# A fused state-space layer: gate by tile over 512 tokens, C scaled by decay before the state's product, the squares' product a step later, the normed sequence kept in DRAM

## What is computed

```python
xn   = layernorm(x)                                   # x: [2, 1024, 512]
proj = xn @ in_proj_w.T                               # gate 4096, x 4096, B 8*128, C 8*128, dt 64
xBC  = silu(causal_conv(proj[x, B, C], 4 taps) + conv_bias)
dt_p = softplus(dt + dt_bias);  dA = exp(-dt_p * exp(A_log))
for t in range(1024):                                 # 64 heads of 64, state 64 x 128 each
    state = state * dA[t] + (dt_p[t] * x[t]) * B[t]
    y[t]  = state @ C[t] + D * x[t]                   # 8 heads share one B and one C
yn   = y * rsqrt(mean(y**2 over 512) + eps) * norm_weight * silu(gate)
s    = yn @ out_proj_w.T
g    = silu(xn @ (W + lora).T + bias)
out  = x + s * g
```

## Time and profile before

| | before |
|---|---|
| median of 3 executions | 1965.25 us (1963.15 to 1968.01) |
| the profiled execution, its own time | 1964.76 us |
| its span, first to last instruction | 1963.0 us |
| granted TensorE clock, mean | 0.983 |
| TensorE (PE) busy | 1849.3 us, 94% |
| VectorE (DVE) busy | 1628.2 us, 83% |
| GpSimd (POOL) busy | 1119.6 us, 57% |
| ScalarE (ACT) busy | 825.4 us, 42% |
| DMA | 185.16 MB, mean 94 GB/s |

### The profile page before, as it was taken

The page is one execution under the profiler, slowest core; times in us unless marked ns, Lnnn a source line. Parts: engine busy times, 40 slices in busy tenths (PEclk is TensorE's granted clock), DMA queues, the critical chain, the costliest instruction groups (busy, mean ns, idle before and its releaser), DMA issues.

```text
span 1963.0 us, 31108 instructions
## 1 busy us (share of the span) xinstructions
PE 1849.3 (94%) x11576; PEld 1527.0 (78%) x11576; DVE 1628.2 (83%) x2000; ACT 825.4 (42%) x1814; POOL 1119.6 (57%) x1145
## 2 busy tenths in 40 slices
PE   7968999999999999999897999999999999999997
PEld 5756888888888887878775888888888888788885
DVE  6758888888888888888875988888888888888896
ACT  4854343444435343434423434443443535344431
POOL 4125555664756555665665756565565555566467
PEclk9988999999999999999998999999999999999998
DMA  6232214242232224232244331314223221423233
GB/s 212 86 100 72 88 50 134 65 118 72 74 103 81 86 65 121 79 113 77 77 154 130 102 103 53 115 65 119 81 79 105 81 83 53 135 65 97 66 91 123
DMA packets 142566, 185.16 MB, mean 94 GB/s; under 512 B 11856, under 2 KB 89040, under 8 KB 142416
## 3 DMA queue, kind: packets, MB, share of 16 engines
q1 hardware_dynamic: 141376, 183.02, 30.9%
q10 hardware_dynamic: 1040, 0.16, 0.0%
HBM read 173.17 MB, written 9.97 MB: 93 GB/s over the span
## 4 chain that ended last, share of the span: by engine, by line
PE 53%; DVE 19%; issue 12%; POOL 9%; ACT 4%; DMA 2%; SPq 0%; POOLq 0%; DVEq 0%; ACTq 0%
PE ps_conv L1086 8%; PE ps_conv L1089 7%; DVE xc L746 5%; PE ps_conv L1092 5%; PE ps_gate L1089 3%; PE ps_gate L1086 3%; PE ps_y L1243 3%; PE ps_out L1086 3%; PE ps_out L1089 3%; DVE decay L854 3%; PE ps_s L1236 3%; PE ps_gate L1092 2%; PE ps_cs L1215 2%; PE ps_out L1092 2%; DVE ycs L834 2%
## 5 line engine op out<-in xcount | busy, mean ns | idle before, releaser
L746 DVE SCALAR_TENSOR_TENSOR xc<-ps_conv,convw_sb,xc 128x511 f32<-128x511 f32 (+2 forms) x576 | 429.7, 746 | 22.6 <-ACT xc L542 9.0
L914 DVE TENSOR_TENSOR decay<-decay,ps_s 128x1024 f32<-128x1024 f32 x128 | 156.0, 1219 | 210.5 <-PE ps_s L1272 210.4
L854 DVE TENSOR_TENSOR_SCAN decay<-decay,eye 128x1024 f32<-128x1024 f32 x128 | 327.8, 2561 | 1.0 <-DMA decay<-decays_d 1.0
L654 ACT ACTIVATE square<-ps_y 128x512 f32<-128x512 f32 x128 | 76.7, 599 | 511.8 <-DVE ps_y L872 511.8
L548 ACT ACTIVATE xc<-xc 128x512 f32<-128x512 f32 x192 | 121.3, 632 | 400.6 <-DVE xc L746 400.3
L1047 POOL TENSOR_TENSOR state<-state,total_bc 128x512 f32<-128x512 f32 x96 | 101.6, 1059 | 316.9 <-DVE state L861 176.5
L1026 POOL TENSOR_TENSOR skip<-skip,ycs 128x512 f32<-128x512 f32 x112 | 150.1, 1340 | 231.6 <-DVE ycs L834 228.8
L1086 PE MATMUL ps_conv<-xn_hi,wconv_hi 128*128 128x512 f32 x768 | 229.3, 420 | 12.4 <-ACT xn_hi L596 10.3
L1089 PE MATMUL ps_conv<-xn_hi,wconv_lo 128*128 128x512 f32 x768 | 209.7, 395 | 0.0
L1031 POOL TENSOR_TENSOR rstd_col<-mean_square,half 128x1 f32<-128x1 f32 x128 | 183.4, 1433 | 0.0
L1243 PEld LDWEIGHTS ps_y<-decay,dtx 128*64 128x64 f32 x2048 | 109.2, 136 | 90.8 <-issue 90.8
(11 more groups left out here) (199 smaller groups left out, 4064.2 us busy)
## 6 DMA issues: line engine op xcount, KB each, us to landing
decay<-decays_d SPq DMA_DIRECT2D x128, 512.0 KB, 5.1
stage<-w_in_t SPq DMA_DIRECT2D x32, 1024.0 KB, 6.4
prefix_bc<-rows_d SPq DMA_DIRECT2D x224, 128.0 KB, 4.8
stage<-w_out_t SPq DMA_DIRECT2D x16, 1024.0 KB, 6.9
stage<-w_in_t SPq DMA_DIRECT2D x32, 256.0 KB, 3.3
out_sum<-hidden SPq DMA_DIRECT2D x16, 256.0 KB, 4.8
ffn_d<-sgate SPq DMA_DIRECT2D x16, 256.0 KB, 2.0
next_x<-hidden SPq DMA_DIRECT2D x16, 256.0 KB, 4.1
```

The source lines that it names most:

```text
L746: e.scalar_tensor_tensor(acc[:, d:], ps[:, 0:BLK - d], convw_sb[:, tile, TAPS - 1 - d:TAPS - d], acc[:, d:], ALU.mult, ALU.add).then_inc(S ...
L854: e.tensor_tensor_scan(d[:, :], d[:, :], eye8[:, :, :].rearrange("p h i -> p (h i)"), 0.0, ALU.mult, ALU.add).then_inc(S["scan"], 1)
L914: e.tensor_tensor(by_head(d[:, :]), by_head(d[:, :]), ps_s[:, 0:P].unsqueeze(1).to_broadcast([P, GH, P]), ALU.mult).then_inc(S["M"], 1)
```

## The change

- **Gate**: one call is one channel tile over 512 tokens, 12 matmuls of 512 columns, with the weights split by channel tile. Step 0 makes four calls, then each step one, until the last at step 124. `sgate` is one buffer of 4 x 4 tiles, written by channel tile and read by chunk; the two roles of its axes alternate.
- **State's product**: GpSimd multiplies the fetched prefix rows (broadcast to all 128 partitions for 8 heads) by C, 1024 elements, a step ahead; TensorE then adds state times this in `ps_y`, with 64-wide weights as in the decay product. The bank `ps_cs`, `ycs`, VectorE's product with the prefix and GpSimd's second sum go.
- **`xw`** is made from `turned_x` in PSUM and `last` (dt times decay to the end, 8 elements) rather than from `dtx` and the decay triangle. The update moves to its own step, after the gate; `xw` and `b_tok` have one buffer.
- **Squares' product**: of `u`, not `m`, after the products into `ps_y`. It, B's transpose and C B share a new bank `ps_g`.
- **Normed sequence**: the split second sequence is stored to DRAM before the loop (16 DMAs of 256 KB) and fetched back in steps 57 to 63; the norming in the loop goes.
- Orders: GpSimd makes skip at the end of its step and the weights' splits are spread differently; output weights are fetched two steps earlier; the last rate part is at step 3, not 2.

The diff, cut to its core:

```diff
+def gated(i):
+
+    return range(0, CPB) if i == 0 else range(i + CPB - 1, min(i + CPB, N))
...
+        xn_d = nc.dram_tensor("xn_d", [2, NCH, P, KT, P], F32).ap()
...
-        xw = [sb(f"xw{i}", [P, GC]) for i in range(2)]
-        b_tok = [sb(f"b_tok{i}", [P, NS]) for i in range(2)]
-        ycs = sb("ycs", [P, GC])
+        xw = sb("xw", [P, GC])
+        b_tok = sb("b_tok", [P, NS])
+        last = sb("last", [P, GH, 1])
         square = sb("square", [P, GC])
         square_sum = sb("square_sum", [P, P])
-        sgate = [sb(f"sgate{i}", [P, XT, 2 * P]) for i in range(2)]
-        prefix_bc = [sb(f"prefix_bc{i}", [P, GC]) for i in range(2)]
+        sgate = sb("sgate", [P, CPB, CPB, P])
+        cpre = [sb(f"cpre{i}", [P, GH, P]) for i in range(2)]
...
-                w.wait_ge(S["cs"], k - 1)
+                b, c, k, g = batch(i), i % NCH, later(i) - 1, group(i) % GROUPS
+                w.wait_ge(S["mm_in"], i - 1)
                 w.wait_ge(st_rows[b, c // CPB], 16)
-                pairs = rows_d[b, c, group(i) % GROUPS * GH:(group(i) % GROUPS + 1) * GH, :].rearrange(
-                    "(t two) i -> two t i", two=2)
-                for half_no in range(2):
-                    e.dma_start(prefix_bc[k % 2][half_no * HD:(half_no + 1) * HD, :].rearrange("p (t i) -> p t i", t=XT),
-                                pairs[half_no].partition_broadcast(HD)).then_inc(landed_rows[k % 2], 16)
...
+                e.dma_start(cpre[k % 2][:, :, :].rearrange("p h i -> p (h i)"),
+                            rows_d[b, c, g * GH:(g + 1) * GH, :].rearrange("h i -> (h i)").partition_broadcast(P)
+                            ).then_inc(landed_rows[k % 2], 16)
...
+            def keep_normed(c):
+
+                w.wait_ge(S["hi"], c + 1)
+                w.wait_ge(S["lo"], c + 1)
+                w.wait_ge(st_xn[c % CPB], 32 if c >= CPB else 0)
+                for part, xn in enumerate((xn_hi, xn_lo)):
+                    e.dma_start(xn_d[part, c], xn[:, :, chunk_cols(c)].bitcast(F32)).then_inc(st_xn[c % CPB], 16)
+
+            def fetch_normed(c):
+                w.wait_ge(S["mm_gate"], N // 2 - NCH + (c // CPB + 1) * CPB)
+                w.wait_ge(S["mm_conv"], (NB // 2 - NBLK + 1 + c // CPB) * MT)
+                w.wait_ge(st_xn[c % CPB], 64)
+                for part, xn in enumerate((xn_hi, xn_lo)):
+                    e.dma_start(xn[:, :, chunk_cols(c)].bitcast(F32), xn_d[part, c]).then_inc(landed_xn[c // CPB], 16)
...
+                if 0 <= i - TURN < NCH:
+                    reload_prefix(i)
+                    blk, r = divmod(i - TURN, CPB)
+                    for c in ((0, 1), (2,), (3,), ())[r]:
+                        fetch_normed(blk * CPB + c)
...
+            def split_gate(g, tiles):
                 w.wait_ge(landed_stage[0], 32 + 32 * g)
-                w.wait_ge(S["mm_gate"], 2 * NCH * g)
                 if g == 0:
                     w.wait_ge(S["mm_ffn"], KT + TOK)
-                split_hi(wgate_hi, staged(0, GC), range(KT), S["hi_gate"])
+                for t in tiles:
+                    w.wait_ge(S["mm_gate"], NCH * g - CPB + t + 1 if g > 0 else 0)
+                    e.activation(wgate_hi[:, :, chunk_cols(t)], staged(0, GC)[:, :, chunk_cols(t)],
+                                 ACT.Copy).then_inc(S["hi_gate"], 1)
...
+                for k in gated(i):
+                    w.wait_ge(S["mm_gate"], k + 1)
+                    w.wait_ge(S["yg"], k - CPB + 1 if k >= CPB else 0)
+                    if k < CPB:
+                        w.wait_ge(ffn_st[0], 16 * NCH)
+                        w.wait_ge(ffn_st[1], 16 * NCH)
+                    e.activation(gate_slot(k), turns(ps_gate), ACT.Silu).then_inc(S["sgate"], 1)
...
-                if 0 <= m < N and cm > 0:
-                    k = later(m) - 1
-                    w.wait_ge(S["mm_cs"], k + 1)
-                    w.wait_ge(landed_rows[k % 2], 32 * (k // 2 + 1))
-                    w.wait_ge(S["base"], k)
-                    w.wait_ge(S["ffn_act"], TOK)
-                    e.tensor_tensor(ycs[:, :], ps_cs[:, :], prefix_bc[k % 2][:, :], ALU.mult).then_inc(S["cs"], 1)
...
+                    if c < NCH - 1:
+                        w.wait_ge(S["scan"], i + 1)
+                        w.wait_ge(S["xw"], inner(i) - 1)
+                        e.tensor_tensor(last[:, :, :], by_head(d[:, :])[:, :, P - 1:P], step_size.unsqueeze(2),
+                                        ALU.mult).then_inc(S["last"], 1)
+                        w.wait_ge(S["last"], inner(i))
+                        w.wait_ge(S["mm_u"], inner(i) - 1)
+                        e.tensor_tensor(by_head(xw[:, :]), by_head(turned_x[:, :]),
+                                        last[:, :, :].to_broadcast([P, GH, HD]), ALU.mult).then_inc(S["xw"], 1)
+                if 0 <= m < N:
+                    w.wait_ge(S["mm_in"], m + 1)
+                    w.wait_ge(S["skip"], m + 1)
+                    e.tensor_tensor(ps_y[:, :], ps_y[:, :], skip[:, :], ALU.add).then_inc(S["y"], 1)
...
+                if i < N and i % NCH > 0:
+                    k = later(i) - 1
+                    w.wait_ge(landed_rows[k % 2], 16 * (k // 2 + 1))
+                    w.wait_ge(S["silu"], conv_no(i // CPB, XT + 1) + 1)
+                    e.tensor_tensor(cpre[k % 2][:, :, :], cpre[k % 2][:, :, :],
+                                    xc[i // CPB % 2][:, XT + 1, block_cols(i % NCH)].unsqueeze(1).to_broadcast(
+                                        [P, GH, P]), ALU.mult).then_inc(S["cpre"], 1)
...
-                cols = slice(k // 2 % (NCH // 2) * 2 * P, (k // 2 % (NCH // 2) + 1) * 2 * P)
-                ready, group_no = gate_ready(k), k // NCH
+                t, blk, group_no = k % XT, k // XT % NBLK, k // NCH
                 w.wait_ge(S["biased"], TOK)
                 w.wait_ge(S["sgate"], k)
-                w.wait_ge(S["hi_gate"], KT * (group_no + 1))
-                w.wait_ge(S["hi"], ready)
-                for t in range(2):
-                    passes(ps_gate[:, t * 2 * P:(t + 1) * 2 * P],
-                           weights(wgate_hi, wgate_lo, chunk_cols(k % 2 * 2 + t)), xn_cols(cols), KT,
-                           lambda: w.wait_ge(S["lo_gate"], KT * (group_no + 1)), lambda: w.wait_ge(S["lo"], ready),
-                           S["mm_gate"])
+                w.wait_ge(S["hi_gate"], XT * group_no + t + 1)
+                w.wait_ge(S["hi"], TOK)
+                w.wait_ge(S["lo"], TOK)
+                if k >= N // 2:
+                    w.wait_ge(landed_xn[blk], 32 * CPB)
+                passes(ps_gate[:, :], weights(wgate_hi, wgate_lo, chunk_cols(t)),
+                       xn_cols(slice(blk * BLK, (blk + 1) * BLK)), KT,
+                       lambda: w.wait_ge(S["lo_gate"], XT * group_no + t + 1), lambda: None, S["mm_gate"])
...
-                    for t in range(XT):
-                        c_state = e.matmul(ps_cs[:, t * P:(t + 1) * P], before[:, t * P:(t + 1) * P],
-                                           xc[m // CPB % 2][:, XT + 1, block_cols(cm)], start=True, stop=True,
-                                           skip_group_check=True)
-                    c_state.then_inc(S["mm_cs"], 1)
...
+                    mx, dx = decay[m % 3], dtx[m % 2]
                     w.wait_ge(S["M"], m + 1)
-                    w.wait_ge(S["pt"], 3 if i < 3 else 4)
-                    if cm < NCH - 1:
-                        at = (inner(m) - 1) % 2
-                        w.wait_ge(S["b_tok"], inner(m))
-                        w.wait_ge(S["xw"], inner(m))
-                        e.matmul(ps_s[:, :], b_tok[at][:, :], xw[at][:, :], start=True, stop=True).then_inc(S["mm_u"], 1)
-                    mx, dx = decay[m % 3], dtx[m % 2]
                     w.wait_ge(S["biased"], TOK)
                     w.wait_ge(S["dtx"], m + 1)
                     w.wait_ge(S["lo2"], m)
-                    for h in range(GH):
-                        rows, cols = slice(h % 2 * HD, (h % 2 + 1) * HD), slice(h // 2 * P, (h // 2 + 1) * P)
-                        mixed = e.matmul(ps_y[rows, cols], dx[:, h * HD:(h + 1) * HD], mx[:, h * P:(h + 1) * P],
-                                         start=True, stop=True, skip_group_check=True)
+                    if cm > 0:
+                        w.wait_ge(S["state"], inner(m - 1))
+                        w.wait_ge(S["cpre"], later(m))
+                        before, c_left = state[(gm + cm - 1) % 2], cpre[(later(m) - 1) % 2]
+                    for two in range(0, GH, 2):
+                        for h in (two, two + 1):
+                            y_h = ps_y[h % 2 * HD:(h % 2 + 1) * HD, h // 2 * P:(h // 2 + 1) * P]
+                            mixed = e.matmul(y_h, dx[:, h * HD:(h + 1) * HD], mx[:, h * P:(h + 1) * P], start=True,
+                                             stop=cm == 0, skip_group_check=True)
+                        if cm > 0:
+                            for h in (two, two + 1):
```

(26 more changed lines are left out.)

355 lines of the change are left out of this document (139 added, 216 removed).

## The result

| | before | after |
|---|---|---|
| median of 4 executions of each on the same chip | 1964.82 us | 1867.92 us |
| ratio, 95% interval | | 0.9507 (0.9490 to 0.9523) |
| span of the profiled execution | 1963.0 us | 1866.3 us |
| granted TensorE clock, mean | 0.983 | 0.99 |
| TensorE busy | 1849.3 us | 1799.7 us |

The kernel is 97 us faster. I had forecast 1899 and a range from 1880 to 1936, so the sign was right and the size too small by 31 us: the time lies outside the range.

The account below looks back on a forecast made before the run. TensorE's queue was taken as the bound, VectorE close behind. Steady groups -28.6, change of batch -34.9, start +2, first group -6.9, end +3 sum to -65.4: 1964.8 to 1899 us, range 1880 to 1936.

Parts of the forecast that it names:

- the content of TensorE's step: TensorE's matmul time: 15.15 us a step before; state's product +0.21 us a step, gate 0.12 off.
- I leave 1.0 us of waits a group: TensorE's waits left in a steady group of eight steps: 1.0 us, between 0.3 and 3.7.
- the two signs of being wrong: Decay product waits for VectorE in more than two steps a group, or a step's two products exceed 2.6 us together.
- 3.7 us of waits lose their named cause: Steady group: the squares' product, a step later, no longer waits for y, square and GpSimd's sums.
- GpSimd's load: GpSimd's busy time in a steady group: from 65.3 to about 74 us, with C times decay at 2.5.
- The change of batch: Group where the batch changes: norming in the loop goes, 3 us left for late GpSimd; 147.3 to 112.4, -34.9 us.
- Rival B: Change of batch keeps some 20 us of wait, SP's queue standing behind a store or the totals: 1920 us, chance 0.08.
- Start and end: Before the first attention product: +2 us on 137.4; last group, its steps set by GpSimd: +3 on 100.6.
- The first group: First group of eight steps: two thirds of its 10.3 us extra idle time goes, 126.9 to 120, -6.9 us.
- A: VectorE's decay times (C B) or the sums stay late as often; steady group stays at 111.6: 1928 us, chance 0.13.
- C: C times decay on GpSimd and VectorE's scan block each other: +3.2 us a group, 1945 us, chance 0.05.
- D: Half-width attention products run at 0.102 us a record, not 0.064: +1.4 us a step, 2033 us, chance 0.04.

Follow-up runs that it names:

- b_update_old: Changed kernel with the state's update put back between the output product and the attention products, a step later, as before the change: 1851.6 us, ratio 0.9430.
- m_b_between: b_update_old with B's transpose moved from ahead of the early conv to between the gate and the second conv: 1865.7 us, ratio 0.9494.
- i_before_sums_ahead: Kernel before the change, with only GpSimd's two sums of squares moved ahead of the state's decay: 1965.0 us, ratio 0.9993.
- c2_sums_first: Changed kernel with the squares' product back in its own step and GpSimd's two sums ahead of its splits and C times decay: 1959.7 us, one run.
- o_best: b_update_old with GpSimd's skip ahead of the state's decay and the very last squares' product ahead of the last output product: 1851.8 us, ratio 0.9421.

## Why the prediction missed

**The step that failed is the content of TensorE's step: it was mis-sized, 0.33 us too long in the step with two convs, and this is most of the miss.** I had 15.15 + 0.21 - 0.12 = 15.24; without waits it is 14.91. By the starts in b_update_old, against my terms: both attention products 1.90 for 2.06 (-0.16: I took 1.03 twice, but a run of such records pays for its two ends once, 0.27 and 0.32 us for its first and last four records where four others take 0.22; the second 16 add 0.87 to 0.89, as the steps of 14.02 without the state's product and 14.91 with it show too); gate 2.72 for 2.76; second conv 2.73 for 2.83, of which m_b_between gives half to the order; first conv 2.83 for 2.86; C B product 0.14 for 0.22; squares' product and transpose 0.31 for 0.25; output product 2.89 for 2.87. Steps with one conv are 0.20 shorter than forecast. Over eight steps, less the parts that two of them lack, that is 1.85 us: content 106.56 where I had 107.9 + 1.5 - 1.0 = 108.4.

**"I leave 1.0 us of waits a group" was right in size by luck** (107.6 - 106.56 = 1.04), with the wrong wait. From one decay times C B to the next VectorE takes 13.15 us, as forecast (13.2), but it begins the step right behind the C B product and not 1.1 to 1.5 us behind it, for which no row of before spoke: the one at 513.37 of the earlier trace rows begins after a wait of 1.66 us for the C B product. So it comes 1.0 late, not 2, inside the limit of 1.6, and the decay product doesn't wait. The update does: the change moves it into its own step, and I didn't ask what its new place asks of VectorE. Neither of the two signs of being wrong that I had named came, and the time was still outside the range.

**"3.7 us of waits lose their named cause"** was true. The chain that I had named, y, square and sums, fits i_before_sums_ahead, where GpSimd's order alone gave nothing, and by c2_sums_first the delay is worth 5.0 us in the changed kernel. GpSimd's load I had too high, 74 us a group for 67.4: C times decay takes 2.39, near the 2.5 forecast, but the power -1/2 now takes 0.84 us in the mean where it took 1.43 (with 2.5 in 57 of its 128 places).

**The change of batch**: 112.4 forecast, 107.6 measured, with two errors behind a fair number. Norming was 18 and not the 32.7 us that I took off for it; the order of the finished output's fetches and sums, which I didn't price at all, 13; and GpSimd's lateness, for which I left 3 us, doesn't show after the change (107.60 is a steady group's length). The remaining 1.8 of the 4.8 are content. Rival B, SP's queue behind a store, didn't come, but a queue that stands was at work in the kernel before, behind a fetch.

**Start and end**: +2 and +3 forecast, -0.2 and -1.2 measured. At the start the forecast is missed by 2.2, about as much as that stretch differs from run to run (135.7 to 138.2). At the end "its steps are GpSimd's" was right: its last steps take 11.1 and 10.5 us, and from the fifth step on the last group takes 48.7 us for 46.5 before, 2.3 more where I had 3. But I left its first four steps as they were, where the change gains as it does elsewhere: 50.7 for 54.0. The last squares' product is hidden behind a wait that exists anyway, by o_best. **The first group**: 122.6 for 120. Its first two steps still take 21.9 and 19.4 us; I had given too much of its idle time to the squares.

**The rivals**: A (waits stay) is not what happened. C's mechanism is real: in the step where the update is late it takes 0.8 us from VectorE (how much of the wait is due to that no run shows), and a steady group pays nothing like the rival's 3.2. D's price is real and its condition not met.

## What to carry to other kernels

Price a section by the distance between starts in its new neighbourhood, and a row that you use twice by its second half: the two ends of a run of matmuls are in it once. For every instruction that moves, name what must be ready at the new place and how late its producer can be; here putting one product back behind another, with the same work, was worth 16 us. And when one slow thing goes, look for the second one that it hid: leave the first out by itself, and see what stays.

## What the runs showed of the hardware

Half-width fp32 records go every 0.055 us when successive products alternate between the two halves of the bank's rows and every 0.102 to 0.11 when they don't (1.90 and 3.26 us for 32). A section of 12 matmuls of 512 columns costs 2.72 to 2.73 us behind one of its own kind and 2.83 to 2.84 behind a transpose or the squares' product. GpSimd's product of 1024 elements with a broadcast input takes 2.39 us, and one of 512 elements 3.02 instead of 1.04 when it meets VectorE's scan, whose length it hardly changes (2.44 for 2.28); a tiny VectorE product behind takes 0.82 instead of 0.17. In the step shown GpSimd's product begins 0.26 us after the scan and ends 0.84 after it. In the kernel before without the norming, TensorE's wait of 4.1 us at the batch change came with a granted clock of 0.83 over 20 us, and that step cost 6 us more.
